# v centred by one pair of fp16 products, without the fp32 product with the identity

## The chip, the cores and the metric

The kernel runs on one core of a Trainium2 chip. The metric is the device time of one execution in microseconds (us), as the median of several runs. Engines are named as the profile names them: PE is TensorE's matmul, PEld its weight load, DVE is VectorE, ACT ScalarE, POOL GpSimd, SP the engine that issues most DMAs.

## The reference

32 sequences of 128 tokens of 256 numbers go through two layers. The first is an attention of the mLSTM kind with 8 heads of 32 numbers: q is the layer norm of x, k and v are both the context `ctx`. The second is a mixture of experts, which picks 2 of 8 experts for each token (GELU between two matrices). Cut to what matters here:

```
qh = heads(layernorm(x));  kh = vh = heads(ctx)
D  = exp(log_D - max(log_D))                # from input and forget gates
C  = (qh @ kh.T) / sqrt(32) * D
h  = (C / (normalizer + EPS)) @ vh
hn = (h - mean(h)) / sqrt(var(h) + LN_EPS) * out_w   # mean over the 32 of a head
x1 = x + hn
out = x1 + experts(layernorm(x1))
```

## The kernel before, in words

The kernel has two stages. In the **attention stage** the 32 sequences go in 8 steps of 4 (`SB = 4`, `NSTEP = 8`); a sequence of a step has the index j. In the **expert stage** tiles of 256 rows, sorted by expert, go through two layers of fp16 products on PE.

Every engine has one instruction stream, and in the attention stage its order is written out by hand: `first_steps` for the start, and then `run_steps`, which calls `body(last, step, nxt, after)` five times; four steps are in work at once, and work of a later one stands between pieces of an earlier one. Steps 0 to 3 are prepared in `first_steps`, steps 4 to 7 as `after` of the first four bodies; the fifth body has no `after`.

Since h minus its head's mean is C times (v minus its head's mean), the kernel centres v ahead of the product. What a step goes through, as far as the change touches it:

- SP loads x and ctx of the step (`load_x`, `load_ctx`). `load_ctx` waits for the turns (`s_tq`) and for the centred v (`s_vm`) of the step before, since there is one ctx buffer.
- DVE takes x's statistics (`next_stats`, L1637) and norms (`next_norm`), ACT applies them (`next_normed`, L732).
- PE `turn` (L1142, L1145) turns x and ctx into `scores`. ACT makes the high fp16 half (`turned`, L750), PE subtracts it (`q_left`, L1151), ACT copies the rest as the low half (`q_low`, L755). So `qkT` holds q and k (that is ctx) turned, each as two fp16 halves.
- PE `centre(step, r)` (L1261, L1264), for two sequences each, puts v minus its mean into the bank `pv`: one fp32 product of ctx with the identity (256 columns) and four fp16 products of 128 columns, of the two halves of the turned ctx with the matrix `meanw` (minus 1/32 within a head, else 0), all added up in one place.
- ACT `v_out` (L836) copies that to `vaug` and signals `s_vc`, for which `times_v` waits through `bank_free`.
- PE `gates` (L1187), DVE `gate_bias` (L1666), ACT `log_sigmoid`, DVE `log_f`, PE `log_f_sum` (L1195), DVE `next_a` (L1687), PE `turn_a` (L1201), DVE `running_max` and `split`, PE `turn_max` (L1207), DVE `max_log_decay` (L1727) make the gates of the step.
- PE `decay_args` (L1167 to L1174) and ACT `decay` (L789) make D, PE `scores` (L1221) q times k, DVE `c_of` (L1749) the product C, PE `times_v` (L1276, L1278) h, ACT `h_out` (L809, L810), DVE `h_norm` (L1759), `h_scaled`, `h_weighted`, `x1_of`. `times_v` and `stream` (L1228) also issue products whose result nobody reads.
- The experts' weights are made into fp16 halves beside it: ACT `weights_high` (L801), DVE `weights_low` (L1740).

POOL builds the constant matrices at the start. PE and DVE wait for all of them (`s_cp` of 21) ahead of their first instruction.

Of the kernel before, what the change touches and what calls it, by code (L numbers as in the profile page):

```python
# [5 lines left out]
ALU = mybir.AluOpType  # L6
# [3 lines left out]
F16 = mybir.dt.float16  # L10
# [3 lines left out]
P = 128  # L14
# [33 lines left out]
def build(nc, x, ctx_in, igate_w, igate_b, fgate_w, fgate_b, out_w, gate_w, w1, b1, w2, b2, out):  # L48
    NB, S, D = x.shape
    NH = igate_b.shape[0]  # L50
    DH = D // NH
    HG = P // DH
    KC = D // P
    NE, _, F = w1.shape
    FC = F // P
    SB = 4
# [43 lines left out]
    with ExitStack() as ctx:  # L100
        def sb(name, shape, dt=F32):
            return ctx.enter_context(nc.sbuf_tensor(name, shape, dt))

        def sem(name):
            return ctx.enter_context(nc.semaphore(name))
# [8 lines left out]
        ctxb = sb("ctx_slots", [P, SB, D])  # L114
# [9 lines left out]
        ident = sb("ident", [P, P])  # L124
# [5 lines left out]
        ident_h = sb("ident_bf16", [P, P], BF16)  # L130
        minus_h = sb("minus_ident_f16", [P, P], F16)
        never = sb("minus_big_above", [P, P], BF16)
        meanw = sb("minus_mean_of_head", [P, P], F16)
        pick = sb("pick_head", [3 * G, G], BF16)
        unpick = sb("minus_pick_head", [3 * G, G], BF16)
        runs = sb("a_and_running_max", [3 * G, 2, P])
# [74 lines left out]
        fill = sb("expert_fill", [P, NE])  # L211
# [18 lines left out]
        ps_h = ctx.enter_context(nc.psum_tensor("pv", [P, 512], F32))  # L230
# [21 lines left out]
        s_c0 = sem("zeroed")  # L252
        s_cp = sem("pool_consts")
# [3 lines left out]
        s_mean = sem("mean_steps")  # L257
# [77 lines left out]
        def number(step):  # L335
            return step[0] * 2 + step[1]

        def some(step, n):

            return not (isinstance(step[0], int) and number(step) < n)  # L340
# [80 lines left out]
        with nc.Block() as block:  # L421
# [172 lines left out]
            def _(pool):  # L594
# [3 lines left out]
                pool.memset(tri_s[:, :], 1.0).then_inc(s_c0, 1)  # L598
                for zero in (ident_h, minus_h, never, pick, unpick):
                    pool.memset(zero[:, :], 0.0).then_inc(s_c0, 1)  # L600
                pool.memset(meanw[:, :], -1.0 / DH).then_inc(s_c0, 1)
                pool.wait_ge(s_c0, 9)
                pool.affine_select(out=ident[:, :], in_=ident[:, :], compare_op=ALU.not_equal, fill=1.0,
                                   base=0, pattern=[[-1, P]], channel_multiplier=1).then_inc(s_cp, 1)
                pool.affine_select(out=tri[:, :], in_=tri[:, :], compare_op=ALU.is_ge, fill=0.0,
                                   base=0, pattern=[[1, P]], channel_multiplier=-1).then_inc(s_cp, 1)
                pool.affine_select(out=tri_s[:, :], in_=tri_s[:, :], compare_op=ALU.is_ge, fill=0.0,
                                   base=-1, pattern=[[1, P]], channel_multiplier=-1).then_inc(s_cp, 1)
# [3 lines left out]
                                   base=0, pattern=[[1, P]], channel_multiplier=-1).then_inc(s_cp, 1)  # L612
                for to, one in ((ident_h, 1.0), (minus_h, -1.0)):
                    pool.affine_select(out=to[:, :], in_=to[:, :], compare_op=ALU.not_equal, fill=one,
                                       base=0, pattern=[[-1, P]], channel_multiplier=1).then_inc(s_cp, 1)
                for n, (to, one) in enumerate(((pick, 1.0), (unpick, -1.0))):
                    for r in range(3):
                        if r:
                            pool.wait_ge(s_pick[n], r)
                        pool.affine_select(out=to[:, :], in_=to[:, :], compare_op=ALU.not_equal, fill=one,  # L620
                                           base=-G * r, pattern=[[-1, G]],
                                           channel_multiplier=1).then_inc(s_pick[n], 1)
                heads = meanw[:, :].rearrange("p (k e) -> p k e", k=HG)
                pool.affine_select(out=heads, in_=heads, compare_op=ALU.is_ge, fill=0.0, base=0,
                                   pattern=[[-DH, HG], [0, DH]], channel_multiplier=1).then_inc(s_mean, 1)
                pool.wait_ge(s_mean, 1)
                pool.affine_select(out=heads, in_=heads, compare_op=ALU.is_ge, fill=0.0, base=DH - 1,
                                   pattern=[[DH, HG], [0, DH]], channel_multiplier=-1).then_inc(s_cp, 1)
                for p in range(2):
                    pool.memset(vaug[:, p, :, :, DH:DH + 1], 1.0).then_inc(s_cp, 1)  # L630
                pool.iota(it_rev[:, :, :], [[0, SB], [-1, NE]], base=NE, channel_multiplier=0).then_inc(s_cp, 1)
# [4 lines left out]
                          channel_multiplier=0).then_inc(s_cp, 1)  # L636
                pool.memset(second_i[:, 0:LATE_BIG + 1], 0.0).then_inc(s_cp, 1)
                pool.iota(second_i[:, LATE_BIG + 1:LATE], [[0, NE // 2 - 1], [-P, 2]], base=P,
                          channel_multiplier=0).then_inc(s_cp, 1)
# [487 lines left out]
            def _(pe):  # L1127
# [121 lines left out]
                def centre(step, r):  # L1249

                    g = number(step)
                    pe.wait_ge(s_ql, g * SB + 2 * r + 2)
                    if r:
                        pe.wait_ge(s_vc, g * 2 + 1)
                    elif some(step, 2):
                        pe.wait_ge(s_hev, g * SB - SB)
                    elif some(step, 1):
                        pe.wait_ge(s_vc, g * 2)
                    for n in range(2):
                        j = 2 * r + n  # L1260
                        pe.matmul(ps_h[:, n * D:n * D + D], ident[:, :], ctxb[:, j, :], start=True, stop=False)  # L1261
                        for c in range(KC):
                            for a in range(2):
                                ins = pe.matmul(ps_h[:, n * D + c * P:n * D + c * P + P], qkT[:, step[1], j, a, KC + c, :],  # L1264
                                                meanw[:, :], start=False, stop=(c == KC - 1 and a == 1))
                    ins.then_inc(s_vm, 1)

                def times_v(step, j):
# [64 lines left out]
                def body(last, step, nxt, after):  # L1333
# [40 lines left out]
                    if after is not None:  # L1374
                        centre(after, 0)
                        q_left(after, 2)
                        q_left(after, 3)
# [11 lines left out]
                    if after is not None:  # L1389
                        centre(after, 1)  # L1390
# [19 lines left out]
                def first_steps():  # L1410
# [7 lines left out]
                    q_left(S0, 2)  # L1418
                    q_left(S0, 3)
                    centre(S0, 0)  # L1420
                    gates(S0)
                    centre(S0, 1)
# [809 lines left out]
```

## Time and profile before

| | |
|---|---|
| median of 3 runs | 648.44 us (647.25 to 649.98) |
| profiled execution: its own time | 651.1 us |
| its span, first to last instruction | 649.1 us |
| mean granted PE clock, of full speed | 0.986 |
| PE busy over the span | 611.4 us, 94% |
| DVE busy | 487.2 us, 75% |
| ACT busy | 323.4 us, 50% |
| POOL busy | 193.7 us, 30% |

Busy times are shares of the whole span, over two stages with different limits. The profiled execution takes 2.0 us more than its span, and 2.7 us more than the median of the runs.

### The profile page before, as it was taken

The page shows a single profiled execution, that of the slowest core. Times are in us where ns is not written, and L with a number is a line of the kernel's source. Part 1 is how long each engine was busy: PE and PEld are TensorE (multiplying, and loading weights), DVE is VectorE, ACT ScalarE, POOL GpSimd, SP SyncE. Part 2 cuts the span into 40 slices and gives each one's busy share as a digit, 9 for nine tenths or more (in the row PEclk, how much of TensorE's full clock was granted, in tenths as well). Part 3 has the DMA queues.
Part 4 walks back from the last instruction along what each step waited for, and adds up shares of the span by engine and source line. Part 5 has one row for each costly group of instructions (what it writes and reads, how often), then busy time and mean ns, then how long its engine had stood idle before and what let it go on. Part 6 is the DMA issues. An engine that isn't in the chain of part 4 may idle for free. (4 is left out here: it accounts for less than half of the span.)

```text
span 649.1 us, 20273 instructions
## 1 busy us (share of the span) xinstructions
PE 611.4 (94%) x6736; PEld 526.6 (81%) x6737; DVE 487.2 (75%) x1330; ACT 323.4 (50%) x767; POOL 193.7 (30%) x185
## 2 busy tenths in 40 slices
PE   1799999999999899999999999999999999999995
PEld 1567777777777668998988988888989888989994
DVE  2546988999999898995888967666676757575684
ACT  2677888897988747544432323233232323232341
POOL 3000002242433424235345523232222323232333
PEclk9898998999999999999999999999999999999998
DMA  4443635475655626233464432323132323243510
GB/s 143 134 127 118 209 99 187 147 238 194 220 166 142 198 91 231 70 73 92 75 186 108 70 68 38 65 36 65 33 62 33 66 33 66 67 119 81 141 34 2
DMA packets 56044, 70.22 MB, mean 108 GB/s; under 512 B 5584, under 2 KB 50832, under 8 KB 55840
## 3 DMA queue, kind: packets, MB, share of 16 engines
q1 hardware_dynamic: 42560, 51.80, 26.3%
q0 software_dynamic: 13296, 17.32, 14.7%
q8 instruction: 49, 0.80, 0.5%
q14 instruction: 27, 0.22, 0.1%
q10 hardware_dynamic: 112, 0.08, 0.0%
HBM read 41.50 MB, written 24.92 MB: 102 GB/s over the span
## 5 line engine op out<-in xcount | busy, mean ns | idle before, releaser
L1059 ACT ACTIVATE decay_slots<-scores,b_turned 128x256 f32<-128x256 f32 (+1 forms) x312 | 124.4, 451 | 241.2 <-PE scores L1545 235.1
L1545 PE MATMUL scores<-x_slots,w_halves 128*128 128x256 f16 (+1 forms) x1760 | 193.7, 266 | 0.0
L1545 PEld LDWEIGHTS scores<-x_slots,w_halves 128*128 x1760 | 165.2, 98 | 17.3
L662 POOL DMA_INDIRECT expert_rows<-xf_rows,slot_i x64 | 71.9, 1124 | 211.8 <-issue 107.0
L1559 PE MATMUL pv<-w_halves,decay_slots 128*128 x864 | 97.6, 273 | 0.0
L684 POOL DMA_INDIRECT out_rows<-v_centred_and_one,row_ids x36 | 58.3, 1619 | 129.2 <-DVE v_centred_and_one L2146 95.7
L1559 PE MATMUL gate_bank<-w_halves,q_and_k_halves 128*128 x840 | 95.0, 273 | 0.0
L1559 PEld LDWEIGHTS pv<-w_halves,decay_slots 128*128 128x128 f16 x864 | 84.4, 98 | 9.7
L1559 PEld LDWEIGHTS gate_bank<-w_halves,q_and_k_halves 128*128 128x128 f16 x840 | 82.0, 98 | 9.5
L684 POOL DMA_INDIRECT out_rows<-work,row_ids x35 | 56.2, 1605 | 104.6 <-DVE work L2146 82.6
L1278 PEld LDWEIGHTS pv<-v_centred_and_one,decay_slots 128*128 128x128 f32 x512 | 63.7, 194 | 1.6
L1278 PE MATMUL pv<-v_centred_and_one,decay_slots 128*128 128x33 f32 x512 | 63.8, 260 | 0.0
L2133 DVE TENSOR_TENSOR decay_slots<-decay_slots 128x512 f16<-128x512 f32 (+1 forms) x80 | 51.2, 640 | 2.8
L2133 DVE TENSOR_TENSOR q_and_k_halves<-decay_slots,q_and_k_halves 128x512 f16<-128x512 f32 (+1 forms) x76 | 49.5, 651 | 2.6
L1740 DVE SCALAR_TENSOR_TENSOR w_halves<-weight_stage,w_halves 128x1024 f16<-128x1024 f32 x32 | 38.9, 1219 | 10.7 <-ACT w_halves L801 10.7
L789 ACT ACTIVATE decay_slots<-turn_bank 128x512 f32<-128x512 f32 x64 | 38.3, 598 | 8.6 <-PE turn_bank L1174 8.4
L1749 DVE SCALAR_TENSOR_TENSOR decay_slots<-scores,decay_slots 128x1024 f32<-128x1024 f32 x32 | 39.1, 1221 | 2.0 <-PE scores L1221 2.0
L2122 DVE CAST x_slots<-turn_bank 128x512 f16<-128x512 f32 (+1 forms) x39 | 25.1, 643 | 18.6 <-PE scores L1545 15.9
L1276 PE MATMUL pv<-minus_big_above,ident_bf 128*128 128x240 bf16 x128 | 34.8, 272 | 2.8 <-ACT work L810 1.7
L801 ACT ACTIVATE w_halves<-weight_stage 128x1024 f16<-128x1024 f32 x32 | 33.8, 1057 | 3.4 <-DMA weight_stage<-in_L_ffn_w 3.4
L2131 DVE CAST decay_slots<-decay_slots 128x512 f16<-128x512 f32 (+1 forms) x80 | 33.3, 416 | 2.0 <-ACT decay_slots L1059 2.0
L2131 DVE CAST q_and_k_halves<-decay_slots 128x512 f16<-128x512 f32 (+1 forms) x76 | 32.2, 423 | 0.1
(263 smaller groups left out, 864.5 us busy)
## 6 DMA issues: line engine op xcount, KB each, us to landing
weight_stage<-in_L_ffn_w SPq DMA_DIRECT2D x32, 512.0 KB, 4.0
x_slots<-in_x SPq DMA_DIRECT2D x16, 512.0 KB, 4.4
weight_stage<-expert_rows SPq DMA_DIRECT2D x30, 272.0 KB, 3.2
ctx_slots<-in_ctx SPq DMA_DIRECT2D x8, 512.0 KB, 6.0
out_rows<-x_slots SPq DMA_DIRECT2D x8, 512.0 KB
v_centred_and_one<-expert_rows SPq DMA_DIRECT2D x9, 272.0 KB, 3.0
expert_rows<-v_centred_and_one SPq DMA_DIRECT2D x9, 272.0 KB, 3.2
xf_rows<-w_halves SPq DMA_DIRECT2D x4, 512.0 KB, 4.1
```

The lines of the kernel that those rows point to most:

```text
L662: pool.indirect_dma_start(table, bass.IndirectOffsetOnAxis(ap=sloti[:, step[1], j, k:k + 1], axis=0), xfn[:, step[1], j, :], None, bounds_ ...
L684: pool.indirect_dma_start(out_rows, bass.IndirectOffsetOnAxis(ap=ids[:, k, b:b + 1], axis=0), yo[k][:, b, :], None, bounds_check=T - 1, oo ...
L789: act.activation(E[:, j, HG * r:HG * r + HG, :].rearrange("p c s -> p (c s)"), ps_t[:, :], ACT.Exp).then_inc(s_ee, 1)
L1059: ins = act.activation(hf[:, f * R:f * R + tr.rows(0)], ps_s[:, q, n * R:n * R + tr.rows(0)], ACT.Gelu, bias=b1T[:, bass.ds(expert, 1), f] ...
L1276: pe.matmul(ps_h[:, P + P + 16:512], ident_h[:, :], never[:, 0:120].unsqueeze(1).broadcast_to([P, 2, 120]), start=True, stop=True)
L1278: ins = pe.matmul(ps_h[:, h * (DH + 1):(h + 1) * (DH + 1)], E[:, j, k * KC + u, :], vaug[:, step[1], j, h, :], start=True, stop=True)
L1545: ins = pe.matmul(o, w, xh[:, tr.slot(0) % 2, b, k, 0:tr.rows(0)], start=(n == 0), stop=(n == 3 * KC - 1))
L1559: ins = pe.matmul(ps_y[k % 2][:, c * D:(c + 1) * D], hh[k % 2][:, a, f, c * P:(c + 1) * P], w, start=(f == 0 and n == 0 and c == 0), stop= ...
L1740: dve.scalar_tensor_tensor(out=lo, in0=stage[:, half, :], scalar=W_SCALE, in1=hi, op0=ALU.mult, op1=ALU.subtract).then_inc(s_lo, 1)
L1749: dve.scalar_tensor_tensor(out=c, in0=ps_s[:, :, 0:KC * P], scalar=QK_SCALE, in1=c, op0=ALU.mult, op1=ALU.mult).then_inc(s_cm, 1)
L2131: dve.tensor_copy(hi, src).then_inc(s_hhi, 1)
L2133: dve.tensor_tensor(lo, src, hi, ALU.subtract).then_inc(s_hh, 1)
```

## The change

The matrix `meanw` gets 1 minus 1/32 on its diagonal and a new name, so that the halves of the turned ctx times it give v minus its mean at once. The fp32 product with the identity goes; the first of the four fp16 products of a sequence now opens the sum. POOL fills the diagonal with one more instruction, behind one more wait on its own work. Nothing else is moved: all waits and signals of PE stay where they are.

```diff
-        meanw = sb("minus_mean_of_head", [P, P], F16)
+        centring = sb("one_minus_mean_of_head", [P, P], F16)
...
-                pool.memset(meanw[:, :], -1.0 / DH).then_inc(s_c0, 1)
+                pool.memset(centring[:, :], -1.0 / DH).then_inc(s_c0, 1)
...
                 pool.affine_select(out=heads, in_=heads, compare_op=ALU.is_ge, fill=0.0, base=DH - 1,
-                                   pattern=[[DH, HG], [0, DH]], channel_multiplier=-1).then_inc(s_cp, 1)
+                                   pattern=[[DH, HG], [0, DH]], channel_multiplier=-1).then_inc(s_mean, 1)
+                pool.wait_ge(s_mean, 2)
+                pool.affine_select(out=centring[:, :], in_=centring[:, :], compare_op=ALU.not_equal,
+                                   fill=1.0 - 1.0 / DH, base=0, pattern=[[-1, P]],
+                                   channel_multiplier=1).then_inc(s_cp, 1)
...
                     for n in range(2):
                         j = 2 * r + n
-                        pe.matmul(ps_h[:, n * D:n * D + D], ident[:, :], ctxb[:, j, :], start=True, stop=False)
                         for c in range(KC):
                             for a in range(2):
                                 ins = pe.matmul(ps_h[:, n * D + c * P:n * D + c * P + P], qkT[:, step[1], j, a, KC + c, :],
-                                                meanw[:, :], start=False, stop=(c == KC - 1 and a == 1))
+                                                centring[:, :], start=(c == 0 and a == 0),
+                                                stop=(c == KC - 1 and a == 1))
```

## Rows read from the trace of the kernel before

**Rows 1.** The page, part 1: busy time of the engines over the span.

```profile
PE 611.4 (94%) x6736; PEld 526.6 (81%) x6737; DVE 487.2 (75%) x1330; ACT 323.4 (50%) x767; POOL 193.7 (30%) x185
```

**Rows 2.** Windows: one body, expert stage; columns PE, PEld, DVE, ACT, POOL, clock.

```profile
160.24:187.64 27.40, 25.87 (x375) 20.95 (x376) 25.74 (x76) 23.56 (x57) 9.44 (x10) 1.00 0.64 198
...
250.00:649.00 399.00, 390.87 (x3791) 351.94 (x3789) 286.64 (x747) 138.16 (x337) 136.22 (x95) 0.99 0.35 74
```

**Rows 3.** Waits of all engines in 132.85:215.04: who, for whom, us, times, longest.

```profile
PE scores L1142 <- DVE decay_slots L1749: 3.1, 3, 1.0
...
PE scores L1221 <- DVE decay_slots L1749: 1.6, 4, 0.4
...
DVE square_sum L1759 <- ACT work L810: 0.6, 3, 0.2
```

**Rows 4.** Waits of DVE in 20:105, the first steps.

```profile
DVE max_log_d L1727 <- PE gate_bank L1207: 5.9, 1, 5.9
DVE log_f_sum L1687 <- PE gate_bank L1195: 4.8, 2, 4.3
...
DVE decay_slots L1749 <- PE scores L1221: 2.0, 2, 1.8
DVE square_sum L1759 <- ACT work L810: 0.5, 1, 0.5
```

**Rows 5.** Groups by line and form on PE: the fp32 product.

```profile
L1261 PE MATMUL pv<-ctx_slots,ident 128*128 128x256 f32 x64 | 20.2, 397 | 0.0
```

**Rows 6.** Timeline, PE, one `centre` in a body: start, length, line.

```profile
177.76 0.59 PE L1261 MATMUL pv<-ctx_slots,ident 128*128 128x256 f32 x2
178.19 0.39 PE L1264 MATMUL pv<-minus_mean_of_head,q_and_k_halves 128*128 128x128 f16 x4
178.41 0.65 PE L1261 MATMUL pv<-ctx_slots,ident 128*128 128x256 f32 x2
178.90 0.39 PE L1264 MATMUL pv<-minus_mean_of_head,q_and_k_halves 128*128 128x128 f16 x4
```

**Rows 7.** Timeline, DVE, step 0's gates: start, length, line, idle before.

```profile
22.17 1.23 DVE L1740 SCALAR_TENSOR_TENSOR w_halves<-weight_stage,w_halves 128x1024 f16<-128x1024 f32 x1 [4.64 <-ACT w_halves L801]
23.32 0.22 DVE L1666 SCALAR_TENSOR_TENSOR gates<-gate_bank,gate_bias_rows 128x64 f32<-128x64 f32 x1
```

**Rows 8.** Timeline, all engines, around `centre` of step 1.

```profile
35.85 1.60 ACT L755 ACTIVATE q_and_k_halves<-scores 128x512 f16<-128x512 f32 x3
...
38.10 0.51 PE L1221 MATMUL scores<-q_and_k_halves 32*128 32x128 f16 x24
...
38.67 1.23 DVE L1749 SCALAR_TENSOR_TENSOR decay_slots<-scores,decay_slots 128x1024 f32<-128x1024 f32 x1 [1.83 <-PE scores L1221]
...
39.81 1.40 DVE L1637 BATCH_NORM_STATS2 bn_parts<-x_slots 128x6 f32<-128x256 f32 x4
```

**Rows 9.** DMA issues in 35:36, step 2's x (issued at 35.33): us to landing.

```profile
x_slots<-in_x SPq DMA_DIRECT2D x1, 512.0 KB, 4.0
```

**Rows 10.** Timeline, PE, `times_v` of step 1, sequence 1.

```profile
73.56 0.26 PE L1276 MATMUL pv<-minus_big_above,ident_bf 128*128 128x240 bf16 x1 [0.43 <-DVE decay_slots L1749]
```

**Rows 11.** Timeline, the start: POOL's last matrix, DVE's and ACT's first waits.

```profile
6.05 0.31 POOL L627 TENSOR_SCALAR_AFFINE_SELECT minus_mean_of_head<-minus_mean_of_head 128x128 f16<-128x128 f16 x1
...
7.38 1.41 DVE L1637 BATCH_NORM_STATS2 bn_parts<-x_slots 128x6 f32<-128x256 f32 x4 [7.25 <-POOL xf_rows L642]
...
13.39 1.06 ACT L801 ACTIVATE w_halves<-weight_stage 128x1024 f16<-128x1024 f32 x1 [3.40 <-DMA weight_stage<-in_L_ffn_w]
```

**Rows 12.** Windows: two stretches with a lower PE clock; columns as in rows 2.

```profile
108.84:112.25 3.41, 3.20 (x17) 3.15 (x17) 3.02 (x9) 3.38 (x8) 1.09 (x2) 0.50 0.62 157
...
50.81:54.22 3.41, 3.41 (x23) 2.20 (x15) 0.35 (x3) 2.72 (x6) 0.00 (x0) 0.50 0.04 14
```

**Rows 13.** Waits of all engines in 105:132.85, the first body.

```profile
DVE max_log_d L1727 <- PE gate_bank L1207: 1.5, 1, 1.5
...
PE scores L1142 <- DMA ctx_slots<-in_ctx: 1.2, 1, 1.2
```

More of the change, by code:

```diff
@@ L622, in _ @@
                                            channel_multiplier=1).then_inc(s_pick[n], 1)
-                heads = meanw[:, :].rearrange("p (k e) -> p k e", k=HG)
+                heads = centring[:, :].rearrange("p (k e) -> p k e", k=HG)
                 pool.affine_select(out=heads, in_=heads, compare_op=ALU.is_ge, fill=0.0, base=0,
```

## The prediction

> **What bounds the kernel now.** The page's first part comes first: PE is busy 94% of the span, the next engine, DVE, 75% [rows 1]. That is a mean over two stages, so the windows by stage come next [rows 2]. In the expert stage, 399 us long, PE is busy 390.87 and DVE 286.64: PE bounds it, and the change has nothing there. In one body of the attention stage, 27.40 us long, PE is busy 25.87 and DVE 25.74: by this view the two are level. So the waits decide [rows 3]. Over three bodies, 82.2 us, DVE waited for another engine 0.6 us in all, and for ACT; PE waited 3.1 + 1.6 = 4.7 us, and both times for DVE's `c_of`. What DVE still lacks to 27.40, 27.40 - 25.74 = 1.66 us a body, is short gaps between its own instructions, most of which need the result of the one before. **In the bodies DVE sets the pace and PE has slack.** All three of these bodies last 27.4 us.
>
> The first steps are another matter [rows 4]. There DVE waits for PE: 5.9 us for `turn_max`, 4.8 us for `log_f_sum`, 2.0 us for `scores`. A shorter PE can show there.
>
> **The change part by part.** *Removed:* 32 fp32 products, two records each, 64 in the trace, 20.2 us busy [rows 5]. Records of PE overlap, so a product's price is the distance of its start to that of the next line: 178.19 - 177.76 = 0.43 and 178.90 - 178.41 = 0.49 us [rows 6]. One `centre` loses 0.92 us, a step 1.84, the 8 steps 14.7 us of PE's time. The four fp16 products stay as they are; that one of them now opens the sum is no operation of its own. Where the 14.7 us go is the whole question.
>
> *Steps 4 to 7 (four bodies, 7.4 us): nothing.* DVE hides it: PE gets sooner to the two places where it waits for `c_of` [rows 3], and waits longer. If that cover were gone, a body could fall to DVE's 25.74 at most, 1.66 us.
>
> *Step 0: nothing.* The gates of step 0 are read by DVE at 23.32, straight behind a weights' instruction (22.17) that had waited 4.64 us for ACT [rows 7]; sooner gates would wait there. Late next is the same DVE instruction.
>
> *Step 1: 0.5 us.* Here `centre` stands right ahead of `scores` of step 0, and DVE waits 1.83 us for these scores [rows 8]. They could start 0.92 us sooner than 38.10, but they need the last low half of step 1, which ACT ends at 35.85 + 1.60 = 37.45. So they start at about 37.55, 0.55 sooner. DVE's next instruction after `c_of` is step 2's statistics at 39.81, and x of step 2, issued at 35.33, takes 4.0 us [rows 9]: 39.33 at the earliest, 0.48 sooner. From there ACT and DVE pass it on as a chain (norm, `decay`, `v_out`, weights, `times_v`). The second `centre` of the step saves PE 0.92 us more, which end at `times_v`, since that waits for `v_out`, which stands in ACT's queue behind the same chain. I take 0.5 us; between 0 (the chain has another gate that I overlooked) and 1.9 (0.5 and 1.4 more), for the following reason. From 50.81 to 54.22 the granted clock is 0.50, the 1.2 GHz level [rows 12]. There DVE waits 4.3 us at once for `log_f_sum` [rows 4] behind PE's work. Were this stretch to run at 2.4 GHz, its 3.4 us of PE work would take half, 1.7 less; about 1.4 of them stand ahead of `log_f_sum`.
>
> *Steps 2 and 3 (3.7 us): nothing.* PE meets a wait for DVE at 73.56 [rows 10], behind both `centre`s of step 2, and all that it does sooner ends there; those of step 3 stand beside a DVE without waits. DVE's waits for PE that are left are 0.2 and 0.5 us [rows 4] and come from PE's work behind 73.56. Bound: 0 to 0.7 us.
>
> *POOL:* one more `affine_select` with its wait. The like one took 0.31 us [rows 11]; with the wait for its forerunner to end I take 0.4. DVE's first instruction, at 7.38, waits for POOL's last, so the statistics of step 0 come 0.4 us later. That is hidden: ACT waits 3.40 us for the first weights, until 13.39, and only behind them applies the norm. Without that cover it would cost 0.4 us.
>
> *Queues:* SP's `load_ctx` waits for `s_vm`, which now comes sooner in steps 0 to 3, so ctx of steps 1 and 2 may be loaded up to about 1 us sooner. In the bodies SP stands behind weights that DVE frees. PE needs neither sooner. Nothing else is moved.
>
> *PE's clock:* with more slack PE is busy less. What it costs if the clock falls stands with the rivals; I take 0, since the three bodies before ran at 1.00 with waits of 1.0 us at a time [rows 2, 3].
>
> *Sum:* -0.5 us. The profiled execution has a span of 649.1 us, own time 651.1, so this goes to 648.6 and 650.6; it stood 2.7 us over the median of the runs. From the median, 648.44 - 0.5 = 647.9 us. Its own range: below, 648.44 - 1.9 - 0.7 = 645.8, and half of the 1.2 us by which the lowest run lay under the median, 645.2; above, no gain, 0.4 for POOL, and the 1.5 us of the highest run over the median, 650.4.
>
> **The rivals.**
>
> *PE does bound the attention stage.* For it: 25.87 against 25.74 us a body [rows 2], and PE's queue holds the gate of nearly everything. Then each of four bodies falls to DVE's busy time, 4 x 1.66 = 6.6 us, and step 1 adds 0.5: 641.3 us. Against it: DVE doesn't wait [rows 3]. Chance 0.05.
>
> *The first steps pass on more.* For it: DVE waits 4.8 + 2.0 + 0.5 = 7.3 us for PE there, and what PE loses in steps 1 to 3 is 3 x 1.84 = 5.5 us [rows 4, 6]. All of it through: 642.9 us; half: 645.7. Against it: the wait at 73.56 and ACT's low halves [rows 8, 10]. Chance 0.07.
>
> *Slower: PE's clock falls in the bodies.* Place: PE's longest wait in a body, for `c_of` ahead of `turn`, 1.0 us [rows 3], behind which come `times_v` and `turn_max`, for which DVE waits next. In the first body PE waited 1.2 us at the same place (there for ctx, at 109), the clock fell to 0.50, the 1.2 GHz level, from 108.84 to 112.25, and DVE then waited 1.5 us for `turn_max` [rows 12, 13]. Longer waits by up to 1.8 us a body may bring that to the other three bodies: 3 x 1.5 = 4.5, so 648.44 - 0.5 + 4.5 = 652.4 us. It decides once PE loses more in such a stretch than it has gained since its last wait for DVE. Against it: the body runs at 1.00 with the same place, and the removed products stand elsewhere; the slack in front of other waits takes up part. Chance 0.08.
> The Trainium skill, page "TensorE: Matmul & The Clock Gate", section "Why this matters for your kernels", asks that TensorE have no long idle gap between bursts of matmuls, or its rate drops. By that rule no fall would come here and the time would be the forecast's, for PE's waits in a body are short; the trace differs, with a fall around a wait of 1.2 us, and so this rival keeps its chance.
>
> That the product doesn't go can't well be: it has its own line in the trace.
>
> **How the numbers follow.** A measurement of this kernel can tell some 0.5%, 3.2 us, from no change. Forecast (no change within that): 0.80, at 647.9. Of it 0.02 lie below 645.2. Faster: 0.05 + 0.07 + 0.02 = 0.14. Slower: 0.08. Same: 0.78. For 8 in 10 the range takes the forecast's own range and, below, half of the second rival: 644.8 to 650.4. Left out are the first rival, the far half of the second and the clock's.
>
> **What would show it.** L1261 has no row left; PE's busy time falls, and its waits for `c_of` grow by some 1 to 1.9 us a body. The distance from body to body stays 27.4 us: that is the step on which the forecast rests, and 27.0 or less would make it wrong. DVE's wait for `scores` of step 0 falls from 1.83 to about 1.3 us. The start of the bodies, now at 132.85 for the second, comes about 0.5 us sooner, and so does the expert stage, unless a stretch at 0.50 is added or lost. A clock row of 0.50 in the bodies would show the third rival.

## The result: 1.8% slower, and the profile after

The median went from 648.68 us (4 runs, 647.25 to 649.98) to **661.39 us** (4 runs, 656.18 to 662.82): a ratio of 1.018, interval 1.0122 to 1.0241. The forecast was 647.9 us and no change, so the prediction was wrong. The kernel before was measured again with every group of experiments below; its median there was 649.4 to 651.3 us. The changed kernel in 12 more runs came to 658.98 us, with 651.31 for the kernel before: slower again, by less (interval 1.0013 to 1.0107). These 12 runs spread far wider than those of the kernel before, from 648.7 to 667.3 us; the interval of a comparison leaves out runs more than 1.5% over the kernel's own fastest, so I set the median of all runs beside it.

The page after, part 1, against [rows 1]:

```profile
PE 614.2 (93%) x6672; PEld 525.6 (80%) x6673; DVE 487.4 (74%) x1330; ACT 322.9 (49%) x767; POOL 194.9 (30%) x186
```

64 records of PE are gone, as announced, and PE is busy *longer*, 614.2 us for 611.4. Fewer products with more busy time means slower products. The windows show where (columns as in [rows 2]; the clock is the third number from the end). First the changed kernel (its own time 661.7 us, span 659.5):

```profile
20.00:60.00 40.00, 31.84 (x358) 24.90 (x358) 19.57 (x54) 22.55 (x51) 0.00 (x0) 0.70 0.36 103
60.00:105.00 45.00, 40.34 (x556) 30.89 (x556) 36.80 (x93) 35.66 (x80) 0.00 (x0) 0.92 0.44 141
105.00:133.00 28.00, 27.25 (x317) 21.52 (x316) 22.96 (x70) 22.15 (x55) 9.78 (x9) 0.82 0.63 192
170.51:197.91 27.40, 24.89 (x370) 19.54 (x374) 25.75 (x76) 23.47 (x57) 9.81 (x10) 1.00 0.60 198
250.00:650.00 400.00, 399.12 (x3886) 359.12 (x3886) 293.17 (x773) 143.49 (x350) 137.01 (x96) 1.00 0.36 79
```

and the first three stretches of the kernel before:

```profile
20.00:60.00 40.00, 34.27 (x414) 26.79 (x414) 22.43 (x61) 27.06 (x59) 0.00 (x0) 0.87 0.41 123
60.00:105.00 45.00, 43.52 (x644) 34.26 (x642) 40.09 (x108) 37.97 (x92) 1.14 (x1) 1.00 0.44 139
105.00:133.00 28.00, 26.39 (x357) 21.53 (x359) 24.72 (x73) 22.76 (x55) 7.97 (x9) 0.94 0.63 202
```

A body and the expert stage run at 1.00, as before. In the first 133 us PE's granted clock is lower in each of the three stretches, and DVE does less in the same time (54 instructions from 20 to 60 us, where it did 61).

How late that makes the work is read from one DVE instruction that comes once a step, the copy of `log_f_sum`. Timeline of DVE, changed kernel, steps 0 to 3 (start, length, line, idle before and releaser), and the group of all eight with its first and last start:

```profile
25.58 0.19 DVE L1691 COPY log_f_sum<-gate_bank 128x32 f32<-128x32 f32 x1 [0.73 <-PE gate_bank L1199]
57.07 0.19 DVE L1691 COPY log_f_sum<-gate_bank 128x32 f32<-128x32 f32 x1 [6.66 <-PE gate_bank L1199]
81.14 0.19 DVE L1691 COPY log_f_sum<-gate_bank 128x32 f32<-128x32 f32 x1 [0.89 <-PE gate_bank L1199]
118.98 0.18 DVE L1691 COPY log_f_sum<-gate_bank 128x32 f32<-128x32 f32 x1
...
L1691 DVE COPY log_f_sum<-gate_bank x8: 178/181/192, 25.6 to 227.4; 128x32 f32<-128x32 f32 x8
```

and the kernel before:

```profile
26.39 0.19 DVE L1687 COPY log_f_sum<-gate_bank 128x32 f32<-128x32 f32 x1 [0.50 <-PE gate_bank L1195]
53.87 0.19 DVE L1687 COPY log_f_sum<-gate_bank 128x32 f32<-128x32 f32 x1 [4.25 <-PE gate_bank L1195]
76.68 0.19 DVE L1687 COPY log_f_sum<-gate_bank 128x32 f32<-128x32 f32 x1
108.66 0.18 DVE L1687 COPY log_f_sum<-gate_bank 128x32 f32<-128x32 f32 x1
...
L1687 DVE COPY log_f_sum<-gate_bank x8: 180/182/192, 26.4 to 217.2; 128x32 f32<-128x32 f32 x8
```

Step 0 comes 0.8 us *sooner* (not by the removal: e1 below, which has the product back, has it at 25.39); step 1 is 3.2 us late, step 2 4.5, step 3 10.3, and step 7 10.2. The two spans differ by 659.5 - 649.1 = 10.4 us. From step 3 to step 7 both kernels take the same time, 227.4 - 118.98 = 108.4 and 217.2 - 108.66 = 108.5 us: three bodies of 27.4, 27.4 and 24.7 us each, and one that is longer, since each kernel has one short fall of the clock among them. In the kernel before it is the first (29.0 us, [rows 12, 13]), in the changed one the second (29.0 us, below).

The stretches at a granted clock of 0.50 (the 1.2 GHz level), called falls below, of the changed kernel:

```profile
23.88:34.12 10.24, 6.49 (x28) 4.82 (x29) 4.86 (x20) 5.54 (x12) 0.00 (x0) 0.50 0.47 149
34.12:44.36 10.24, 8.25 (x153) 5.90 (x151) 4.51 (x13) 7.98 (x20) 0.00 (x0) 1.00 0.40 105
44.36:58.02 13.66, 13.17 (x109) 10.66 (x107) 5.50 (x14) 6.01 (x13) 0.00 (x0) 0.50 0.28 78
78.50:85.32 6.82, 6.82 (x53) 4.89 (x53) 4.26 (x18) 3.98 (x11) 0.00 (x0) 0.50 0.71 242
105.80:116.04 10.24, 10.24 (x95) 8.25 (x94) 7.55 (x24) 5.21 (x18) 2.14 (x2) 0.50 0.64 201
```

The second row is the stretch at 1.00 ahead of the worst fall. The four at 0.50 make 41.0 us; the kernel before had 13.7 in the same part (26.93 to 33.75 and the two of [rows 12]). Later there are two short ones, 146.76 to 150.17 and 232.09 to 235.51, and in both kernels one of some 4 us at the very end, behind PE's last product. In the fall of 44.36 PE is busy 13.17 of 13.66 us: it is not starved, it works slowly, and DVE waits for it, 6.66 us for the `log_f_sum` above instead of 4.25. What PE did before that fall (timeline; idle before and releaser in brackets):

```profile
42.29 0.39 PE L1171 MATMUL turn_bank<-pick_head,three_parts 96*128 96x512 bf16 x1 [1.05 <-ACT decay_slots L793]
...
43.72 0.28 PE L1280 MATMUL pv<-minus_big_above,ident_bf 128*128 128x240 bf16 x1 [0.60 <-ACT v_centred_and_one L840]
```

From 34.12 on it had waited 0.34 (at 37.16, a row of it further below), 1.05 and 0.60 us, each time for ACT. The kernel before waited only once in this part, 0.56 us for `times_v`, and not for the decay arguments: its fp32 products stood in that time, PE was busy 10.06 of the 10.25 us from 33.75 to 44.00, and the clock stayed at 1.00.

### The profile page after: what moved, and what is told of

It reads as the page before. It is cut to its first block and busy times, and to the rows that moved or that the text cites. A ratio compares the mean times of both kernels' runs of the same rounds, so it can differ in the third digit from the quotient of the medians.

```text
span 659.5 us, 20147 instructions
## 1 busy us (share of the span) xinstructions
PE 614.2 (93%) x6672; PEld 525.6 (80%) x6673; DVE 487.4 (74%) x1330; ACT 322.9 (49%) x767; POOL 194.9 (30%) x186
## 5 line engine op out<-in xcount | busy, mean ns | idle before, releaser
L1282 PEld LDWEIGHTS pv<-v_centred_and_one,decay_slots 128*128 128x128 f32 x512 | 69.8, 210 | 1.5
L1282 PE MATMUL pv<-v_centred_and_one,decay_slots 128*128 128x33 f32 x512 | 69.9, 272 | 0.0
L1280 PE MATMUL pv<-minus_big_above,ident_bf 128*128 128x240 bf16 x128 | 36.3, 284 | 4.0 <-ACT work L814 1.4
```

Source lines behind the costliest of these rows:

```text
L1280: pe.matmul(ps_h[:, P + P + 16:512], ident_h[:, :], never[:, 0:120].unsqueeze(1).broadcast_to([P, 2, 120]), start=True, stop=True)
L1282: ins = pe.matmul(ps_h[:, h * (DH + 1):(h + 1) * (DH + 1)], E[:, j, k * KC + u, :], vaug[:, step[1], j, h, :], start=True, stop=True)
```

## The experiments

**Theory 1:** the removed products had kept PE active in the first steps; without them its clock is at the lower level there for longer, on work that sets the end. **Theory 2:** the time went to something else of the change (another order of waits, the later constant, the earlier ctx loads). The prediction's own rival, a fall of the clock in the bodies, is a third. Each kernel below is the changed one, as it is or with added products whose results nobody reads; g_before_idle alone is the kernel before with such products. The times of all:

| kernel | runs | median | lowest to highest | median clock | ratio to before, 95% |
|---|---|---|---|---|---|
| changed kernel, again (after_again) | 12 | 658.98 | 648.68 to 667.25 | 0.970 | 1.0013 to 1.0107 |
| e1_fp32_unused | 10 | 649.80 | 647.25 to 653.58 | 0.989 | 0.9944 to 1.0015 |
| e2_fill_all | 10 | 652.10 | 648.12 to 655.43 | 0.986 | 0.9974 to 1.0045 |
| e3_fill_first_steps | 10 | 652.59 | 648.15 to 657.81 | 0.984 | 0.9990 to 1.0074 |
| e4_fill_bodies | 10 | 656.35 | 650.43 to 665.52 | 0.972 | 1.0023 to 1.0109 |
| f_s01 | 10 | 651.58 | 648.26 to 658.88 | 0.986 | 0.9980 to 1.0058 |
| f_s23, then f_s23_more | 4, 12 | 655.34, 655.09 | 647.34 to 664.29 | 0.975 | 1.0012 to 1.0094 |
| f_idle | 10 | 654.14 | 646.10 to 660.85 | 0.981 | 1.0006 to 1.0102 |
| g_all | 12 | 652.02 | 649.22 to 655.74 | 0.994 | 1.0002 to 1.0064 |
| g_all6 | 6 | 657.79 | 653.85 to 660.87 | 0.993 | 1.0080 to 1.0180 |
| g_before_idle | 12 | 650.38 | 648.70 to 656.88 | 0.996 | 0.9994 to 1.0064 |
| h_waits | 12 | **646.80** | 645.19 to 649.98 | 0.996 | **0.9923 to 0.9981** |
| h_waits_c2 | 12 | 647.98 | 645.30 to 652.38 | 0.994 | 0.9941 to 1.0002 |

The kernel before had medians of 651.23 (e rows), 651.31 (f rows and after_again), 649.35 (g rows) and 650.32 us (h rows and f_s23_more), with 23 to 31 runs each. The second row of f_s23's interval is that of the 12 runs.

### Putting PE work back in the old place

e1, the very product again, its result overwritten:

```diff
                         j = 2 * r + n
+                        if True:
+                            pe.matmul(ps_h[:, n * D:n * D + D], ident[:, :], ctxb[:, j, :], start=True, stop=True)
                         for c in range(KC):
```

> The changed kernel, with the removed fp32 product (identity times ctx, 256 columns) issued again in its old place, in every step, ahead of the four fp16 products that now overwrite its result. Nothing of the computation changes; the product is unused. Theory 1 (the fp32 products had kept PE active in the first steps; without them PE's clock stands at its lower level there for longer, and that costs the 10 us): about the kernel before, 646 to 650 us, and the half-clock stretches up to 117 us from the start back to some 14 us in sum, where the changed kernel has 45. Theory 2 (the time went to something else of the change: the step's values now wait in another order, the constant is made later, the earlier start of step 1's scores meets something): about the changed kernel, 658 to 663 us.

e2, the same time of PE in bf16 on constants; the kernels for single steps have a condition in place of `True`, e3 `g < 4`, e4 `g >= 4`, f_s01 `g < 2` and f_s23 `2 <= g < 4`:

```diff
                         j = 2 * r + n
+                        if True:
+                            for _ in range(4):
+                                pe.matmul(ps_h[:, n * D:n * D + 2 * P], ident_h[:, :],
+                                          never[:, :].unsqueeze(1).broadcast_to([P, 2, P]), start=True, stop=True)
                         for c in range(KC):
```

> The changed kernel with four bf16 products of 256 columns of constants in place of each removed fp32 product, in every step: the same time on PE (1,024 columns), no fp32 and no read of ctx, result unused and overwritten. Nothing of the computation changes. Theory 1: 646 to 650 us, as any activity of PE would do. Theory 2: 658 to 663 us. A third reading, that it was the fp32 product itself that kept the clock up (four passes of wide data) and not PE's being busy: between, above 652 us.

> The changed kernel with the four bf16 products of 256 columns of constants in steps 0 to 3 alone; steps 4 to 7 as in the changed kernel. Nothing of the computation changes. Theory 1, by which the whole loss arises in the first steps: 646 to 650 us, the same as with the fill in all steps. The prediction's own rival (the clock falls in the three bodies of steps 4 to 7): 655 us or more, about the changed kernel. Theory 2: 658 to 663 us.

> The changed kernel with the four bf16 products of 256 columns of constants in steps 4 to 7 alone; steps 0 to 3 as in the changed kernel. Nothing of the computation changes. Theory 1: no gain, 658 to 663 us, the half-clock stretches of the first 117 us as in the changed kernel. The prediction's own rival (the bodies): 646 to 652 us. Theory 2: 658 to 663 us.

Measured, on one chip: 649.80, 652.10, 652.59 and 656.35 us, with 651.23 for the kernel before. e1 and e2 are back at the kernel before, whatever the product reads; e1's profile has falls of 3.4 us (28 to 32) and 10.2 us (106 to 118), some 14 in sum, as expected. That speaks against theory 2: the later constant is still in both. But the ctx loads, which wait for the end of the centring, and what follows the centring on PE stand later again in them; h_waits, below, has both as the changed kernel does and loses nothing either. e3 is back too: e2 and e3 lie 2 to 3 us above the 646 to 650 us that theory 1 gave, but the kernel before itself lies 1.2 us above them on this chip. e4 is not back: its interval lies above 1, and its runs reach 665.5. Its 656.35 us lies in neither of its two ranges, and these runs don't tell it from the changed kernel's 658.98. So filling the bodies brought nothing that these runs show, and filling the first steps did. The intervals of e3 and e4 overlap, and the two profiles tell more than the medians do: e4's is of its second slowest run, e3's of its second fastest. e4's (own time 662.5 us) has nearly the same windows as the changed kernel:

```profile
20.00:60.00 40.00, 32.17 (x353) 25.39 (x354) 19.25 (x52) 21.95 (x48) 0.00 (x0) 0.68 0.34 103
60.00:105.00 45.00, 41.66 (x521) 32.96 (x520) 33.96 (x79) 33.77 (x76) 0.00 (x0) 0.83 0.43 141
...
L1695 DVE COPY log_f_sum<-gate_bank x8: 178/180/191, 25.4 to 228.2; 128x32 f32<-128x32 f32 x8
```

and e3's (648.4 us) the better ones:

```profile
20.00:60.00 40.00, 33.89 (x438) 27.18 (x435) 24.07 (x65) 27.97 (x61) 0.00 (x0) 0.91 0.45 132
60.00:105.00 45.00, 43.33 (x663) 34.82 (x662) 40.23 (x111) 37.73 (x92) 2.15 (x2) 1.00 0.47 147
...
L1695 DVE COPY log_f_sum<-gate_bank x8: 180/181/192, 25.3 to 214.2; 128x32 f32<-128x32 f32 x8
```

`log_f_sum` of step 7 stands at 228.2 in the one and at 214.2 in the other. The third reading of e2, that only fp32 keeps the clock up, has no support: its 652.10 us lies at the edge of "above 652", and the interval takes in both no change and e1.

### The changed kernel once more, and which steps

> The changed kernel as it is, once more, so that its time stands beside the others on one chip and in more runs. Theory 1 and theory 2 alike: 656 to 663 us, some 1.5 per cent over the kernel before.

> The changed kernel with the four bf16 products of 256 columns of constants before each sequence's centring in steps 0 and 1 alone. Nothing of the computation changes. Theory 1, with the loss where the trace of the changed kernel shows the first two longer half-clock stretches (24 to 58 us from the start, 24 us of them where the kernel before has 10): most of the loss comes back, 648 to 654 us. If each step's fall is its own: half comes back, 654 to 657 us.

> The changed kernel with the same products in steps 2 and 3 alone. Nothing of the computation changes. Theory 1: the stretches from 78 us on go, those of 24 to 58 us stay, and 3 to 6 us of the 10 come back: 653 to 658 us. If falls are only passed on from the first one: no gain, 658 to 663 us.

> The kernel with four bf16 products before each sequence's centring in steps 2 and 3 alone, in more runs (the first four lay from 647.5 to 663.2 us). Nothing of the computation changes. If steps 0 and 1 decide, as their fill alone came out at the time of the kernel before: a median of 655 to 660 us, near that of the changed kernel. If the fill in any two steps does as much: 650 to 653 us.

The changed kernel came to 658.98 us on the same chip. **What its 12 runs tell is the price of the clock.** The fastest, 648.68 us (span 645.6), had a mean clock of 0.990, the slowest, 667.25 (664.8), one of 0.954. As the clock is 1.00 or 0.50, the time at 0.50 is 2 x 0.010 x 645.6 = 12.9 us in the one and 2 x 0.046 x 664.8 = 61.2 us in the other: 19.2 us of span for 48.3 us, **0.4 us for each us at 0.50** (a line through all twelve has 0.38). Nothing here sets the clock by itself, so this is how time goes with the clock from run to run. In the first profile the changed kernel has 41.0 + 3.4 - 13.7 = 30.7 us more of it up to the end of the bodies, 12.3 us by that price, and 9.8 if the lead of 2.5 us that is found below is taken off. Measured were 10.4. A fit over the 112 runs of the kernel before lies on nearly the same line, 641.1 us + 0.44.

f_s01 gave back nearly all: 651.58 us. f_s23 gave back some: 655.09 in 12 runs, between the changed kernel and the one before, and it still reaches 664.3. Its first stretch shows why:

```profile
20.00:60.00 40.00, 31.07 (x395) 24.40 (x395) 23.45 (x61) 26.57 (x59) 0.00 (x0) 0.83 0.43 130
60.00:105.00 45.00, 43.35 (x660) 34.50 (x658) 39.80 (x114) 37.97 (x92) 2.00 (x2) 1.00 0.45 140
```

Its own steps (second row) are at 1.00, the first row stays at 0.83. So steps 0 and 1 weigh most, and the later ones have a share; how large, runs that spread by 17 us don't settle.

### Filling the waits instead

If what counts is that PE is busy, and not the product, then products in its *waits* should do, and cost nothing. f_idle has 22 of them, into the bank that the routing uses later, where the changed kernel's trace shows PE waiting:

```diff
+                    stream_idle(8)
                     log_f_sum(S0)
                     turn_a(S0)
+                    stream_idle(8)
                     decay_args(S0, 0, 0)
...
+                    stream_idle(4)
                     decay_args(S0, 2, 1)
+                    stream_idle(2)
                     times_v(S0, 0)
```

(`stream_idle(n)` issues n products of 512 columns, `ident_h` by `never`, into `ps_x`.)

> The changed kernel without any product before the centring; in its place 8, 8, 4 and 2 bf16 products of 512 columns of constants into a free bank, where the trace of the changed kernel shows PE waiting in the first 44 us (2.57 us ahead of log_f_sum, 2.29 us ahead of the first decay arguments, 1.05 us ahead of the sixth, 0.60 us ahead of the first times v). Nothing of the computation changes. Theory 1: the half-clock stretches of 24 to 58 us get shorter or go, 650 to 655 us; if they go altogether and what follows with them, below the kernel before. Theory 2: 658 to 664 us, the products being only more work.

The profiled run came at 646.10 us, just under the fastest of the 29 of the kernel before in its group (646.11), with a clock of 1.00 from 20 to 60 us. But the ten runs go up to 660.85, with clocks down to 0.967; the profiled run has its one early fall at 70.8 to 74.2 us. So later waits were filled as well, in g_all with the products ahead of the centring besides:

```diff
+                    stream_before(S1, 0, 6)
                     times_v(S1, 0)
...
+                    stream_before(S2, 0, 3)
                     times_v(S2, 0)
...
-                        stream_before(step, 2, 3)
+                        stream_before(step, 2, 7 if step == S2 else 3)
```

> Meant to beat both kernels: the changed kernel with the four bf16 products before each sequence's centring in steps 0 to 3, the 22 products of 512 columns in the waits of the first 44 us, and 6, 3 and 4 more of these in the later waits that the changed kernel's trace shows (1.29 us ahead of times v of step 1, 0.2 and 0.6 us ahead of that of step 2, 1 us ahead of the first body's x turn). All results unused; nothing of the computation changes. Theory 1: all runs so far, of every kernel, lie near one line, span = 641 us and 0.4 us for each us at half clock; with 0 to 10 us at half clock this one gives 643 to 648 us and a narrow spread, under the 651 us of the kernel before. Theory 2: no better than 651 us.

> The same with more of it: six bf16 products in place of four before each sequence's centring, in all steps, and 8, 5 and 6 products in the later waits. All results unused; nothing of the computation changes. Theory 1: 643 to 648 us as well; above the kernel with fewer by up to 1.5 us if the longer products end up on PE's path in the bodies, below it if they hold the clock up in more of the runs. Theory 2: 652 us or more.

> The kernel before, fp32 products and all, with the same products in its waits (22 of 512 columns in the first 44 us, then 6, 3 and 4) and none before the centring. Results unused; nothing of the computation changes. It tells what the removal is worth by itself once the clock is held: theory 1 with the prediction's own sum (step 1 some 0.5 us earlier, all else hidden): 643 to 648 us, within 2 us of the changed kernel so filled. If the removed products cost time of their own: 2 us or more above it.

The clock did what was expected (no stretch at 0.50 in the first 120 us of the three profiled runs, medians of 0.993 to 0.996), the time did not: 652.02, 657.79 and 650.38 us all miss the 643 to 648 us. What I had overlooked is that products ahead of the centring are no filling of waits in these steps: they lie on PE's path. `log_f_sum` of step 7 stands at 215.9 in g_all, 4.0 us behind the 211.9 of h_waits below, which has the same products in the waits and none ahead of the centring; 2.0 of these are there at step 3 (106.46 and 104.49), with no fall so far in either, and 1.6 came with g_all's one fall, at 135.1 to 138.5. In g_all6, with six products in every step, each body also grew by 0.6 us. **Doing it without them:**

> The changed kernel with products of constants in PE's waits alone, none before the centring: the 22 of the first 44 us and the 6, 3 and 4 later ones. Results unused; nothing of the computation changes. Theory 1, with the fall of steps 1 and 2 that the first 22 alone left (70.8 to 74.2 us in the profiled run, more in others by the granted clocks of 0.97) also held: 644 to 649 us, under the kernel before and under the one that also fills before the centring, whose products lengthened PE's path in steps 0 to 3 by some 1.5 us. If products in waits alone can't hold the clock there: 650 to 656 us, spread wide.

> The same with two bf16 products of 256 columns before each sequence's centring in steps 1 to 3 (half of the fill that gave back the loss before, and none in step 0, where PE's path sets the end). Results unused; nothing of the computation changes. Theory 1: 645 to 649 us with few falls. Should the clock need the full product: 650 to 655 us.

h_waits is the changed kernel with the products in the waits alone. It gave **646.80 us, faster than the kernel before (interval 0.9923 to 0.9981)** and with the narrowest spread of all, 4.8 us. Its windows and its group:

```profile
20.00:60.00 40.00, 35.14 (x441) 25.11 (x441) 25.27 (x70) 29.95 (x67) 0.00 (x0) 1.00 0.45 133
60.00:105.00 45.00, 42.29 (x636) 32.53 (x633) 41.20 (x113) 37.40 (x89) 2.15 (x2) 1.00 0.51 163
105.00:133.00 28.00, 25.38 (x371) 19.97 (x371) 25.83 (x76) 24.08 (x59) 10.88 (x10) 1.00 0.64 195
...
34.12:44.36 10.24, 9.76 (x164) 6.91 (x163) 6.41 (x16) 7.37 (x19) 0.00 (x0) 1.00 0.42 107
...
L1703 DVE COPY log_f_sum<-gate_bank x8: 178/180/192, 25.4 to 211.9; 128x32 f32<-128x32 f32 x8
```

1.00 throughout. From 34.12 to 44.36 PE is busy 9.76 us, where it was 8.25 ahead of the changed kernel's worst fall. DVE gets through 70 instructions from 20 to 60 us, where the kernel before did 61 and the changed one 54. Half a product ahead of the centring in steps 1 to 3 (h_waits_c2) adds nothing.

g_before_idle has the same products in its waits *and* the fp32 products. So the pair comes nearest to what the change is worth once the clock is held. DVE's rows in g_before_idle:

```profile
36.87 1.22 DVE L1761 SCALAR_TENSOR_TENSOR decay_slots<-scores,decay_slots 128x1024 f32<-128x1024 f32 x1 [1.84 <-PE scores L1221]
...
51.24 0.19 DVE L1699 COPY log_f_sum<-gate_bank 128x32 f32<-128x32 f32 x1 [3.44 <-PE gate_bank L1195]
...
74.57 0.19 DVE L1699 COPY log_f_sum<-gate_bank 128x32 f32<-128x32 f32 x1 [0.68 <-PE gate_bank L1195]
```

and in h_waits:

```profile
35.99 1.23 DVE L1765 SCALAR_TENSOR_TENSOR decay_slots<-scores,decay_slots 128x1024 f32<-128x1024 f32 x1 [1.24 <-PE scores L1225]
...
49.80 0.19 DVE L1703 COPY log_f_sum<-gate_bank 128x32 f32<-128x32 f32 x1 [2.86 <-PE gate_bank L1199]
...
72.36 0.19 DVE L1703 COPY log_f_sum<-gate_bank 128x32 f32<-128x32 f32 x1
```

0.9, 1.4 and 2.2 us sooner, and 2.5 at step 7 (214.4 and 211.9). The runs differ by 650.38 - 646.80 = 3.6 us, on two chips, and by 4.5 us when each is set against the kernel before on its own chip (1.0 above it and 3.5 below); the rest of that I can't place.

The products in the waits are not free, though. With its clock held at 0.996, g_before_idle is no faster than the kernel before, 650.38 for 649.35 us, and lies some 4.7 us above the line of that kernel's runs. Its row at 74.57 has a wait of 0.68 us for PE, where the kernel before has none (76.68). In h_waits the first body takes 132.35 - 104.49 = 27.86 us, where f_idle, which lacks the four products there, takes 27.39, and DVE waits for PE at `turn_max`, which it does not in f_idle:

```profile
108.73 0.19 DVE L1743 TENSOR_TENSOR max_log_d<-log_f_sum,gate_bank 128x32 f32<-128x32 f32 x1 [0.58 <-PE gate_bank L1211]
```

So the 2.5 us are the lead of one filled kernel over the other. How much of it the removal brings by itself, no run here separates.

## Why the prediction was wrong

- **The step that failed** is "*PE's clock* ... I take 0, since the three bodies before ran at 1.00". It judged the clock by the bodies, where the change brings PE no wait that matters, and left out the first steps, though [rows 12] showed a stretch at 0.50 there in the kernel before, with DVE waiting behind it [rows 4]. I had used that row for a possible *gain* (the 1.9 us bound: the stretch at 2.4 GHz) and not asked what brings more of them. What the runs showed in that step's place is 27.3 us more at 0.50 in the first 117 us (41.0 for 13.7), and with it a loss of 10.4 us in the profiled pair and of 7.7 us between the medians of the repeat (658.98 and 651.31).
- The **slower rival** had the clock and, for one body, the very place, but not its condition, longer waits there: behind PE's wait for `c_of` ahead of `turn`, the clock fell from 146.76 to 150.17, DVE waited 1.73 us for `turn_max`, and that body took 29.0 us. PE's row of that wait and DVE's:

```profile
146.61 0.53 PE L1146 MATMUL scores<-ident,x_slots 128*128 128x128 f32 x2 [1.04 <-DVE decay_slots L1753]
...
151.76 0.19 DVE L1731 TENSOR_TENSOR max_log_d<-log_f_sum,gate_bank 128x32 f32<-128x32 f32 x1 [1.73 <-PE gate_bank L1211]
```

  The wait is 1.04 us, where the three of the kernel before were up to 1.0. It foresaw 1.5 us for each of three bodies; in one of them the clock fell, and the kernel before had lost as much in its first body. The profile of the repeat has no fall in the bodies from 128 us on. The 10.3 us came from where no rival looked: the clock in the first steps.
- *Steps 4 to 7: nothing* was right; bodies without a fall take 27.4 us as before. One sign given for it was wrong: PE's waits for `c_of` did not grow. Waits of PE in 143:225 of the changed kernel, against [rows 3]:

```profile
PE scores L1146 <- DVE decay_slots L1753: 3.1, 3, 1.0
PE scores L1225 <- DVE decay_slots L1753: 1.5, 2, 0.7
PE turn_bank L1171 <- ACT decay_slots L793: 0.7, 3, 0.2
```

  PE idles 27.40 - 24.89 = 2.51 us a body, where it was 1.53: 1.0 us more in short gaps ahead of several lines, and not 1.84. The price of the product was part of that. By the starts of [rows 6] a `centre` took 0.43 + 0.22 + 0.49 + 0.22 = 1.36 us; without the fp32 products its eight fp16 products are one row, busy for 0.61:

```profile
182.55 0.61 PE L1267 MATMUL pv<-one_minus_mean_of_head,q_and_k_halves 128*128 128x128 f16 x8
```

  By starts they cost 0.68 here (to PE's next row at 183.23, 0.07 of it idle), and 0.54 in the first steps (40.19 to 40.73, with no wait behind), and not 2 x 0.22 = 0.44. So a `centre` saves some 0.7 us in a body, where I took 0.92. In the first steps the 0.92 was right: 1.46 us before (41.08 to 42.54), 0.54 now.
- *Step 1: 0.5 us* was right up to where the clock fell. Timeline of the changed kernel:

```profile
35.53 1.57 ACT L759 ACTIVATE q_and_k_halves<-scores 128x512 f16<-128x512 f32 x3
...
37.16 0.51 PE L1225 MATMUL scores<-q_and_k_halves 32*128 32x128 f16 x24 [0.34 <-ACT q_and_k_halves L759]
...
37.73 1.22 DVE L1753 SCALAR_TENSOR_TENSOR decay_slots<-scores,decay_slots 128x1024 f32<-128x1024 f32 x1 [1.23 <-PE scores L1225]
...
39.15 1.41 DVE L1641 BATCH_NORM_STATS2 bn_parts<-x_slots 128x6 f32<-128x256 f32 x4 [0.20 <-DMA x_slots<-in_x]
```

  `scores` waits for ACT's last low half, DVE's wait for them is 1.23 for 1.83, and the statistics start 0.66 sooner, held by the landing of x, all as worked out [rows 8, 9].
- *Steps 2 and 3: nothing, bound 0 to 0.7*: with the clock held, the lead of h_waits over g_before_idle goes on growing from 1.4 us at step 1 to 2.2 at step 2 and 2.5 at step 7. Were all of it the removal's, the sum of 0.5 us was too small by 2 us and the gain lies about at the far bound, 1.9 + 0.7. That is the direction of the rival "the first steps pass on more", half of it; in the changed kernel the clock took it away. Two of the prediction's figures don't come out of its rows: the 7.3 us of that rival count 0.5 us twice or take in a wait for ACT [rows 4], and half of that rival is 645.7 by its own sum, not the 644.8 that the range takes. Neither bears on the result.
- *POOL*: one more row of 0.29 us, and DVE's first instruction at 7.82 for 7.38, 0.44 us later as estimated; ACT still waits 2.22 us for the first weights behind it, so it is hidden.

```profile
6.51 0.29 POOL L630 TENSOR_SCALAR_AFFINE_SELECT one_minus_mean_of_head<-one_minus_mean_of_head 128x128 f16<-128x128 f16 x1
...
7.82 1.41 DVE L1641 BATCH_NORM_STATS2 bn_parts<-x_slots 128x6 f32<-128x256 f32 x4 [7.69 <-POOL xf_rows L646]
...
12.65 1.06 ACT L805 ACTIVATE w_halves<-weight_stage 128x1024 f16<-128x1024 f32 x1 [2.22 <-DMA weight_stage<-in_L_ffn_w]
```

Of the rule cited in the prediction: no wait of PE between 34.12 and 44.36 was longer than 1.05 us, and the clock fell. The Trainium skill, page "TensorE: Matmul & The Clock Gate", section "A second HAM failure mode: psum-queue depth-cycling", tells of a kernel in which short, frequent idle times between groups of matmuls made the clock go up and down. There the groups go through PSUM banks in turn; here PE waited for ACT and DVE, and its clock went up and down (the rows from 23.88 to 116.04). In the two later stretches at 1.00 ahead of a fall, 58.02 to 78.50 and 85.32 to 105.80, PE's longest waits were 1.3 and 0.7 us. Which of the waits brought which fall, no run here separates. I had looked only at the rule on long gaps.

## What to carry to other kernels

Where a stretch of the kernel already shows a lower granted clock, work taken off TensorE ahead of it isn't free time: ask first whether that work was keeping the clock up, and price its loss by rows at either level (here 0.4 us of span for each us at the lower one). Products of constants put into TensorE's waits gave the clock back to the changed kernel (646.8 for 659.0 us, on two chips); more of them on its path held the clock too and cost their own time. In the kernel before, with its fp32 products still in place, they brought nothing (650.4 for 649.4 us). When the mean clock differs from run to run, take ten runs and read the times against the clock before a difference of 1% is believed.

## What the runs showed that I had not expected

- The same program's runs differ by up to 18.6 us (648.68 to 667.25) and the mean granted clock goes with them, from 0.990 to 0.954. The runs of the kernel before stand nearly on one line of span and clock; g_before_idle, g_all and g_all6 lie above it by some 5, 4 and 9 us.
- The longest waits in the 10 us before the worst fall were 1.05 and 0.60 us. The fall then lasted 13.66 us, although PE was busy for 13.17 of these.
